# Conv filters stored in four shifted DRAM copies, so that one 128-partition transfer loads a run of ring units

## The chip, the cores and the metric

One core of a Trainium2 chip runs the whole program. The time is device microseconds of one execution; lower is better.

## The reference, cut to what matters

The input is (4, 512, 16, 32) float32, that is 2048 tokens of 512 values. Four residual layers follow one another: a mixture of 8 experts, and three convolution layers.

```
x = x + experts(_gn(x))        # top 2 of 8: silu(x w1ᵀ) * (x w3ᵀ), then w2ᵀ, weighted
x = x + conv(_gn(x), w3, w7, w15, w_mix)      # three times, each with its own weights
# conv: causal depthwise filters of 3, 7 and 15 taps over the tokens of a batch,
#   outs = [dwconv(x_flat, w) for w in (w3, w7, w15)]; y = concat(outs)
#   regrouped by 96 channels a head, then y @ w_mixᵀ (96 -> 32 channels a head)
```

A depthwise filter of k taps followed by the mix is, for one head and one group of 32 channels, a sum of k products with 32x32 matrices.

## The kernel before, in words

**Experts part.** Rows are gathered into blocks of 128 tokens, sorted by expert; there are 35 blocks, 4 or 5 for an expert. For a block g, TensorE (PE) does 48 matmuls for gate and up (L934), transposes the next block's rows (`next_rows`, L911), then `down` of the block before (L921, L924) and the transposes of `hidden` (L946). The rows of block g+1 are fetched from DRAM by GpSimd's gather ("fetch", L434); VectorE normalises them (L727); PE's L911 waits for that. GpSimd works in order: fetch, then the scatter with addition of an earlier block's result to `acc` (L443, "scatter"), then a wait until that scatter has landed (`added`), and only then the next fetch (after a copy, L432). ScalarE's L540 also waits for that landing before it fills `y_row` again.

All weights are loaded by SyncE (SP) from one queue. In its loop over experts e = 1 to 7 it issues the four w13 chunks (1024 KB each) and the two w2 halves (1024 KB each) of expert e while expert e-1 is at work; chunks 2 and 3 wait until chunks 0 and 1 have landed, the w2 halves until chunks 2 and 3 have. ScalarE (L509) and VectorE (L733) split each chunk into a high and a low part before PE uses it.

**Filters.** In the first block of each expert 1 to 7 VectorE multiplies taps and mix matrices into `filter_sb` (two chunks of 128 partitions x 12,544 bytes), splits them (L524, L763), and SP stores both chunks in DRAM (L376). In SP's program the two stores of expert e come after the w2 loads of e and ahead of the w13 loads of e+1. Partition p of a chunk is row r = p // 4 of unit p % 4; the row holds the lags of the three filters, 32 columns a lag, with zeros around them.

**Convolutions part.** Tokens are split in four phases q, so that 32 channels x 4 phases fill the 128 partitions. A head is computed in three units, each of 2, 3 or 5 windows (3, 7 or 15 taps); a window is three matmuls (L1409, L1410, L1413) whose 128x128 weights lie in `ring`, a ring buffer of 52 windows. Partitions 32q to 32q+31 of a window are the same 32 filter rows, read at an offset that moves by 32 columns with q. `load_filters` issues the loads in the order of the heads; each waits for the tasks that used its place in the ring (`head_done`). A layer has 21 tasks: heads 11 and 12 in two halves (by pair of batches), then ten whole heads, then heads 3, 4, 5 in two halves. SP first loads `rowed` of batches 0 and 1, then head 11's filters, then `rowed` of batches 2 and 3, then all other filters. PE's order in the first tasks: head 11 half 0; head 12 half 0 with a transpose (`turn`) after its first unit and, after its second, `lane_means` of the second pair of batches (L1343), for which VectorE needs that transpose's piece done and then eight `bn_stats` (L1175).

Of the kernel before, what the change touches and what calls it, by code (L numbers as in the profile page):

```python
# [6 lines left out]
P = 128  # L7
BATCH, SEQ, D, F, E = 4, 512, 512, 1024, 8
QUARTERS = SEQ // P
# [18 lines left out]
LAYERS, HEADS, HD = 3, 16, 32  # L28
SCALES = (3, 7, 15)
GROUPS = D // HD  # L30
# [7 lines left out]
SCALE_AT = (0, (SCALES[0] + 8) * HD, (SCALES[0] + SCALES[1] + 16) * HD)  # L38
LAGS = (sum(SCALES) + 8 * len(SCALES)) * HD
CHUNKS_PER_LAYER = GROUPS * HD // P  # L40
CHUNKS = 2 * (E - 1)
FILTERS_FREE = 32


def windows(s):

    return (SCALES[s] + 1) // QUARTERS + 1


def head_units(h):  # L50

    return [divmod(3 * h + m, GROUPS) for m in range(3)]


def head_runs(h):

    runs, taken = [], 0
    for s, j in head_units(h):
        if runs and runs[-1][0] == s:
            runs[-1][2] += 1  # L60
        else:
            runs.append([s, j, 1, taken])
        taken += windows(s)
    return runs
# [36 lines left out]
RING_AT, RING_AFTER, RING_COUNT = [], [], []  # L101
for _i, (_l, _h) in enumerate(HEAD_SEQUENCE):
    _at = RING_AT[-1] + head_windows(HEAD_SEQUENCE[_i - 1][1]) if _i else 0
    if _at + head_windows(_h) > RING:
        _at = 0
    _old = [_n for _n in range(_i)
            if RING_AT[_n] < _at + head_windows(_h) and _at < RING_AT[_n] + head_windows(HEAD_SEQUENCE[_n][1])]
    RING_AT.append(_at)
    RING_AFTER.append(max((_n + 1 for _n, (_layer, _head, _) in enumerate(TASKS)
                           if _old and (_layer, _head) == HEAD_SEQUENCE[_old[-1]]), default=None))  # L110
    RING_COUNT.append((_l + 1) * QUARTERS * len(head_runs(_h)))

BANKS = 5
SCALED = 2
# [16 lines left out]
def build(nc, x, gate_wT, w13T, w2T, taps, mixT, out):  # L131
    f32, f32r, i32, u32 = mybir.dt.float32, mybir.dt.float32r, mybir.dt.int32, mybir.dt.uint32
    ALU, ACT, AX = mybir.AluOpType, mybir.ActivationFunctionType, mybir.AxisListType


    acc = nc.dram_tensor("acc", [TOKENS + P, D], f32).ap()
    filters = nc.dram_tensor("filters", [HD, CHUNKS * P // HD, 2, LAGS], f32).ap()
    with ExitStack() as ctx:
        def sb(name, shape):
            return ctx.enter_context(nc.sbuf_tensor(name, shape, f32))  # L140

        ident = sb("ident", [P, P])
        group_mean = sb("group_mean", [P, P])

        filters_out = ctx.enter_context(nc.semaphore("filters_out"))
        experts_part(nc, x, gate_wT, w13T, w2T, acc, ident, group_mean, taps, mixT, filters, filters_out)
        conv_part(nc, acc, out, filters, filters_out, ident, group_mean)
# [8 lines left out]
def experts_part(nc, x, gate_wT, w13T, w2T, acc, ident, group_mean, taps, mixT, filters, filters_out):  # L156
    f32, f32r, i32, u32 = mybir.dt.float32, mybir.dt.float32r, mybir.dt.int32, mybir.dt.uint32
# [4 lines left out]
    with ExitStack() as ctx:  # L162
# [36 lines left out]
        filter_sb = late_rows[:, 0:4 * LAGS].rearrange("p (i s n) -> p i s n", i=2, s=2)  # L199
# [116 lines left out]

        block = ctx.enter_context(nc.Block(name="experts"))

        def load_w13(eng, e, k):
            eng.dma_start(w13_raw[:, k], w13T[bass.ds(e, 1), k].rearrange("o p t n -> (o p) t n"))\  # L320
               .then_inc(w13_in[k], 16)
# [26 lines left out]
        @block.sync  # L348
        def _(sp):
            for b in range(BATCH):  # L350
                sp.dma_start(rows[:, b * QUARTERS:(b + 1) * QUARTERS, 0:D], x_rows[b]).then_inc(x_in[b], 16)
            for k in range(KD):
                load_w13(sp, 0, k)

            sp.wait_ge(values_done, 1)
            for half in range(2):
                load_w2(sp, 0, half)


            sp.dma_start(taps_sb, taps).then_inc(taps_in, 16)  # L360
            sp.dma_start(mix_sb, mixT).then_inc(taps_in, 16)


            with sp.Fori(1, E) as e:
                for k in range(KD):
                    sp.wait_ge(w13_ok, (e - 1) * KD + k + 1)
                    if k >= 2:
                        sp.wait_ge(w13_in[k - 2], 16 * (e + 1))
                    load_w13(sp, e, k)
                for half in range(2):  # L370
                    sp.wait_ge(w2_ok, (e - 1) * 2 + half + 1)
                    sp.wait_ge(w13_in[KD - 2 + half], 16 * (e + 1))
                    load_w2(sp, e, half)
                for i in range(2):
                    wait_apart(sp, filter_ok, e * 2 + (i - 1), sp_passed)
                    sp.dma_start(filters[:, bass.ds(e * 8 + (4 * i - 8), P // HD)].rearrange("r a s n -> r a (s n)"),  # L376
                                 filter_sb[:, i].rearrange("p s n -> p (s n)")).then_inc(filters_out, 16)

        @block.gpsimd
        def _(pool):  # L380
# [186 lines left out]
        def _(dve):  # L567
# [37 lines left out]

            dve.sem_inc(filters_out, FILTERS_FREE)
            for b in range(BATCH):
# [135 lines left out]
            def after_first(e, g0):  # L743
                split_w2(e, g0)
                if isinstance(e, int):
                    dve.wait_ge(taps_in, 32)
                    dve.wait_ge(filter_zero, 1)
                    return
                dve.wait_ge(filters_out, e * 32 + (FILTERS_FREE - 32))
                for i in range(2):  # L750
                    c = bass.ds(e * 2 + (i - 2), 1)
                    tap = 0
                    for s, k in enumerate(SCALES):
                        at = SCALE_AT[s] + (QUARTERS - 1) * HD
                        last = nc.vector.tensor_tensor(
                            filter_sb[:, i, 1, at:at + k * HD].rearrange("p (k d) -> p k d", d=HD),
                            taps_sb[:, c, tap:tap + k].rearrange("p o k -> p (o k)")[:, :, None].to_broadcast([P, k, HD]),
                            mix_sb[:, c, s, :].to_broadcast([P, k, HD]), ALU.mult)
                        tap += k
                    last.then_inc(product_ok, 1)  # L760
                for i in range(2):
                    dve.wait_ge(filter_hi_ok, e * 2 + (i - 1))
                    nc.vector.tensor_tensor(filter_sb[:, i, 1].bitcast(f32r), filter_sb[:, i, 1], filter_sb[:, i, 0],  # L763
                                            ALU.subtract).then_inc(filter_ok, 1)
# [195 lines left out]
def conv_part(nc, acc, out, filters, filters_out, ident, group_mean):  # L960
    f32, f32r = mybir.dt.float32, mybir.dt.float32r
    ALU, ACT, AX = mybir.AluOpType, mybir.ActivationFunctionType, mybir.AxisListType
    acc_rows = acc[0:TOKENS, :].rearrange("(b p q) n -> b p q n", p=P, q=QUARTERS)
    out_rows = out.rearrange("b (p q) h w -> b p q (h w)", q=QUARTERS)
    filter_rows = filters.rearrange("r j s n -> r (j s) n")

    with ExitStack() as ctx:
        def sb(name, shape, dt=f32):
# [11 lines left out]
        ring = sb("ring", [P, RING * 2 * P], f32r)  # L980
# [24 lines left out]
        ring_in = [sem(f"ring_in{h}") for h in range(HEADS)]  # L1005
# [53 lines left out]
        @block.sync  # L1059
        def _(sp):  # L1060
            def load_rows(b):
                sp.dma_start(rowed[:, b], acc_rows[b]).then_inc(rows_in[b], 16)  # L1062

            def load_filters(i):
                l, h = HEAD_SEQUENCE[i]
                if RING_AFTER[i] is not None:
                    sp.wait_ge(head_done, RING_AFTER[i])
                for s, j0, n, taken in head_runs(h):
                    at, width = (RING_AT[i] + taken) * 2 * P, windows(s) * P
                    for q in range(QUARTERS):  # L1070
                        begin = SCALE_AT[s] + (QUARTERS - 1 - q) * HD
                        sp.dma_start(ring[HD * q:HD * (q + 1), at:at + 2 * n * width].bitcast(f32).rearrange("r (a n) -> r a n", n=width),  # L1072
                                     filter_rows[:, 2 * (l * GROUPS + j0):2 * (l * GROUPS + j0 + n), begin:begin + width]).then_inc(ring_in[h], 16)

            load_rows(0)
            load_rows(1)
            sp.wait_ge(filters_out, FILTERS_FREE + 16 * CHUNKS)
            load_filters(0)
            load_rows(2)
            load_rows(3)  # L1080
            for i in range(1, len(HEAD_SEQUENCE)):
                load_filters(i)

            stores = 0
            for tasks, first, end, bs in STORES:
                sp.wait_ge(placed, tasks)
                for b in bs:
                    sp.dma_start(out_rows[b, :, :, first * HD:end * HD], rowed[:, b, :, first * HD:end * HD]).then_inc(stored, 16)
                    stores += 1
            sp.wait_ge(stored, 16 * stores)  # L1090
# [404 lines left out]
```

## Time and profile before

| what | us |
|---|---|
| median of 3 runs | 1171.56 (1164.51 to 1361.69) |
| the profiled execution | 1166.2 |
| its span, all engines | 1164.3 |
| experts part, up to the first load of `rowed` | 745.5 |
| convolutions part | 419 |

The mean granted clock of PE in the profiled execution was 0.947 of full speed. The span is from the first to the last instruction of the profile; 1.9 us of the execution lie around it.

### The profile page before, as it was taken

What the parts mean: (1) busy time and instruction counts of PE and PEld (TensorE: products, weight loads), DVE (VectorE), ACT (ScalarE), POOL (GpSimd) and SP (SyncE); (2) the same over time, 40 slices, a digit from 0 to 9 for tenths busy, and PEclk for the clock granted to TensorE, in tenths of its full rate; (3) what the DMA queues carried; (4) which work ended last, traced back from release to release, by engine and by line L of the source; (5) the groups of instructions that cost most, each with busy time, mean ns of one, the idle gap of its engine ahead of it and who ended that gap; (6) DMA issues with size and microseconds to landing.
All of it is one profiled execution on the core that took longest, in us unless ns stands there. A gap on an engine that the chain in (4) does not pass through costs nothing. (4 is left out here: it accounts for less than half of the span.)

```text
span 1164.3 us, 14374 instructions
## 1 busy us (share of the span) xinstructions
PE 1060.9 (91%) x5234; PEld 883.5 (76%) x5235; DVE 501.3 (43%) x692; ACT 318.5 (27%) x433; POOL 128.1 (11%) x170
## 2 busy tenths in 40 slices
PE   5588999999999999999999999168999979989998
PEld 3377887887887887887878877158888968888887
DVE  5773163154245263154451452135325952387011
ACT  2403242142243242153431432012301220122112
POOL 2013111211211212111212111000000000000000
PEclk9769999999999999999999999667999989999999
DMA  8208218316415519217338140492998299698993
GB/s 361 82 19 316 48 28 314 76 27 245 138 33 196 185 18 351 39 27 278 105 112 275 27 137 18 128 238 63 205 193 182 47 220 208 127 192 168 204 207 100
DMA packets 66336, 172.72 MB, mean 148 GB/s; under 512 B 8192, under 2 KB 38016, under 8 KB 57280
## 3 DMA queue, kind: packets, MB, share of 16 engines
q1 hardware_dynamic: 58080, 149.19, 45.1%
q0 software_dynamic: 8080, 23.07, 9.4%
q8 instruction: 21, 0.34, 0.1%
q14 instruction: 11, 0.09, 0.0%
q10 hardware_dynamic: 144, 0.02, 0.0%
HBM read 136.15 MB, written 40.30 MB: 152 GB/s over the span
## 5 line engine op out<-in xcount | busy, mean ns | idle before, releaser
L1409 PE MATMUL head_ps<-split,ring 128*128 128x512 f32 (+1 forms) x630 | 225.8, 358 | 18.7 <-DMA ring<-filters 17.2
L1413 PE MATMUL head_ps<-split,ring 128*128 128x512 f32 (+1 forms) x630 | 220.2, 350 | 0.0
L1410 PE MATMUL head_ps<-split,ring 128*128 128x512 f32 (+1 forms) x630 | 219.8, 349 | 0.0
L1409 PEld LDWEIGHTS head_ps<-split,ring 128*128 128x128 f32 x630 | 123.6, 196 | 35.2 <-DMA ring<-filters 17.8
L1413 PEld LDWEIGHTS head_ps<-split,ring 128*128 128x128 f32 x630 | 123.3, 196 | 15.7
L1410 PEld LDWEIGHTS head_ps<-split,ring 128*128 128x128 f32 x630 | 123.7, 196 | 14.9
L921 PE MATMUL y_ps<-w_hi,hT_hi 128*128 128x512 f32 x280 | 117.5, 420 | 1.2 <-ACT hT_hi L534 1.2
L785 DVE TENSOR_TENSOR hidden<-silu,up_ps 128x1024 f32<-128x1024 f32 x35 | 42.7, 1219 | 165.0 <-ACT silu L552 165.0
L921 PE MATMUL y_ps<-w_lo,hT_hi 128*128 128x512 f32 x280 | 113.5, 405 | 0.0
L1236 DVE TENSOR_TENSOR stream<-stream,head_ps 128x512 f32<-128x512 f32 (+1 forms) x63 | 34.1, 557 | 176.2 <-PE head_ps L1413 176.2
L773 DVE TENSOR_TENSOR hT_lo<-hT_ps,hT_hi 128x1024 fp32r<-128x1024 f32 x35 | 42.7, 1221 | 134.0 <-ACT hT_hi L534 134.0
L552 ACT ACTIVATE silu<-gate_ps 128x1024 f32<-128x1024 f32 x35 | 35.9, 1025 | 235.5 <-PE up_ps L934 235.5
L934 PE MATMUL gate_ps<-w_hi,xT_hi 128*128 128x512 f32 x280 | 89.9, 402 | 1.7 <-DVE xT_lo L768 1.7
L443 POOL DMA_INDIRECT acc<-y_row,put x35 | 63.4, 1810 | 214.6 <-ACT y_row L540 206.3
L934 PE MATMUL up_ps<-w_hi,xT_hi 128*128 128x512 f32 x280 | 86.9, 392 | 0.0
L934 PE MATMUL up_ps<-w_lo,xT_hi 128*128 128x512 f32 x280 | 86.8, 391 | 0.0
L934 PE MATMUL gate_ps<-w_lo,xT_hi 128*128 128x512 f32 x280 | 86.7, 391 | 0.0
L934 PE MATMUL gate_ps<-w_hi,xT_lo 128*128 128x512 f32 x280 | 86.6, 391 | 0.0
L934 PE MATMUL up_ps<-w_hi,xT_lo 128*128 128x512 f32 x280 | 86.3, 390 | 0.0
L733 DVE TENSOR_TENSOR w_lo<-w_raw,w_hi 128x2048 fp32r<-128x2048 f32 x32 | 71.9, 2285 | 4.7 <-ACT w_hi L509 4.7
L924 PE MATMUL y_ps<-w_hi,hT_lo 128*128 128x512 f32 x280 | 69.3, 389 | 0.0
L921 PEld LDWEIGHTS y_ps<-w_hi,hT_hi 128*128 128x128 f32 x280 | 55.7, 199 | 12.8 <-issue 1.4
(189 smaller groups left out, 1362.8 us busy)
## 6 DMA issues: line engine op xcount, KB each, us to landing
w_raw<-in_w13T SPq DMA_DIRECT2D x32, 1024.0 KB, 11.5
ring<-filters SPq DMA_DIRECT2D x60, 480.0 KB, 10.4
filters<-rows SPq DMA_DIRECT2D x14, 1568.0 KB, 7.2
w_raw<-in_w2T SPq DMA_DIRECT2D x16, 1024.0 KB, 6.1
ring<-filters SPq DMA_DIRECT2D x84, 192.0 KB, 6.2
ring<-filters SPq DMA_DIRECT2D x48, 288.0 KB, 7.2
rows<-in_x SPq DMA_DIRECT2D x4, 1024.0 KB, 8.1
rowed<-acc SPq DMA_DIRECT2D x4, 1024.0 KB, 12.1
```

Source lines behind the costliest of these rows:

```text
L443: pool.indirect_dma_start(out=acc[:, :], out_offset=bass.IndirectOffsetOnAxis(put[:, 0:1].bitcast(u32), 0), in_=y_row[:, :], in_offset=Non ...
L552: nc.scalar.activation(silu[:, :].rearrange("p (a n) -> p a n", a=2), gate_ps[:, :, :], ACT.Silu).then_inc(silu_ok, 1)
L733: nc.vector.tensor_tensor(w13_lo[:, k], w13_raw[:, k], w13_hi[:, k].bitcast(f32), ALU.subtract).then_inc(w13_ok, 1)
L773: nc.vector.tensor_tensor(hT_lo[:, :, :], hT_ps[:, :, :], hT_hi[:, :, :].bitcast(f32), ALU.subtract).then_inc(hT_ok, 1)
L785: nc.vector.tensor_tensor(hidden[:, :].rearrange("p (a n) -> p a n", a=2), silu[:, :].rearrange("p (a n) -> p a n", a=2), up_ps[:, :, :], ...
L921: nc.tensor.matmul(y_ps[:, :], hT_hi[:, k, :], b[:, k, :], start=(k == 0 and b is w2_hi), stop=False)
L924: last = nc.tensor.matmul(y_ps[:, :], hT_lo[:, k, :], w2_hi[:, k, :], start=False, stop=(k == KF - 1))
L934: last = nc.tensor.matmul(o[:, n, :], a[:, k, :], b[:, k, t, n * 512:(n + 1) * 512], start=(k == 0 and a is xT_hi and b is w13_hi), stop=( ...
L1236: nc.vector.tensor_tensor(x, x, head_ps[n % BANKS][:, columns(pair)], ALU.add).then_inc(summed, 1)
L1409: nc.tensor.matmul(place, kernel_hi, x_hi, start=(u == 0 and a == 0), stop=False)
L1410: nc.tensor.matmul(place, kernel_lo, x_hi, start=False, stop=False)
L1413: last = nc.tensor.matmul(place, kernel_hi, x_lo, start=False, stop=(u == len(units) - 1 and a == windows(s) - 1))
```

## The change

`filters` in DRAM becomes four copies, one for each phase q, each row shifted right by 32q columns. SP stores each of the 14 chunks four times (56 stores of 1568 KB instead of 14), at the same place of its program. `load_filters` then reads all four phases at one column offset, so a run of units is one transfer to 128 partitions instead of four to 32 partitions: 54 transfers instead of 216, with the same bytes and the same contiguous pieces. Counts that are waited for follow.

```
-    filters = nc.dram_tensor("filters", [HD, CHUNKS * P // HD, 2, LAGS], f32).ap()
+    filters = nc.dram_tensor("filters", [QUARTERS, HD, ROW_OF_FILTERS], f32).ap()
...
+        def by_group(q):
+            return filters[q, :, q * HD:q * HD + CHUNKS * P // HD * 2 * LAGS].rearrange("r (a n) -> r a n", n=2 * LAGS)
...
                     wait_apart(sp, filter_ok, e * 2 + (i - 1), sp_passed)
-                    sp.dma_start(filters[:, bass.ds(e * 8 + (4 * i - 8), P // HD)].rearrange("r a s n -> r a (s n)"),
-                                 filter_sb[:, i].rearrange("p s n -> p (s n)")).then_inc(filters_out, 16)
+                    for q in range(QUARTERS):
+                        sp.dma_start(by_group(q)[:, bass.ds(e * 8 + (4 * i - 8), P // HD)],
+                                     filter_sb[:, i].rearrange("p s n -> p (s n)")).then_inc(filters_out, 16)
...
-                    for q in range(QUARTERS):
-                        begin = SCALE_AT[s] + (QUARTERS - 1 - q) * HD
-                        sp.dma_start(ring[HD * q:HD * (q + 1), at:at + 2 * n * width]...,
-                                     filter_rows[:, 2 * (l * GROUPS + j0):2 * (l * GROUPS + j0 + n), begin:begin + width])...
+                    sp.dma_start(ring[:, at:at + 2 * n * width]...,
+                                 filter_rows[:, 2 * (l * GROUPS + j0):2 * (l * GROUPS + j0 + n), SCALE_AT[s]:SCALE_AT[s] + width])...
```

## Rows read from the trace of the kernel before

**Rows 1.** The page, part 1: busy time of each engine.

```profile
PE 1060.9 (91%) x5234; PEld 883.5 (76%) x5235; DVE 501.3 (43%) x692; ACT 318.5 (27%) x433; POOL 128.1 (11%) x170
```

**Rows 2.** Waits of PE: who released it, us in total, times, longest.

```profile
PE xT_ps L911 <- DVE block_row L727: 21.6, 10, 2.9
PE head_ps L1409 <- DMA ring<-filters: 17.2, 3, 7.5
```

**Rows 3.** Timeline of SP in expert 3: start and length in us, issues.

```profile
362.12 2.24 SPq L376 DMA_DIRECT2D filters<-rows  x2
364.93 14.49 SPq L320 DMA_DIRECT2D w_raw<-in_w13T  x4
381.64 4.84 SPq L325 DMA_DIRECT2D w_raw<-in_w2T  x2
```

**Rows 4.** DMA issues at 270.5 to 272.5: count, KB, median us to landing.

```profile
filters<-rows SPq DMA_DIRECT2D x2, 1568.0 KB, 7.4
acc<-y_row,put POOLq DMA_INDIRECT x1, 12.8
```

**Rows 5.** DMA issues at 285.6 to 288, beside weight loads.

```profile
block_row<-in_x,fetch POOLq DMA_INDIRECT x1, 5.3
acc<-y_row,put POOLq DMA_INDIRECT x1, 9.0
```

**Rows 6.** DMA issues at 300.5 to 312, nothing beside them.

```profile
acc<-y_row,put POOLq DMA_INDIRECT x1, 4.8
block_row<-in_x,fetch POOLq DMA_INDIRECT x1, 3.3
```

**Rows 7.** DMA issues at 679 to 680.5, two stores and no weights.

```profile
acc<-y_row,put POOLq DMA_INDIRECT x1, 10.4
```

**Rows 8.** Timeline at 285 to 292: the fetch and PE's L911.

```profile
285.64 1.01 POOL L434 DMA_INDIRECT block_row<-in_x,fetch  x1 [0.82 <-POOL fetch L432]
...
291.75 0.66 PE L911 MATMUL xT_ps<-ident,block_row 128*128 128x128 f32 x4 [0.20 <-DVE block_row L727]
```

**Rows 9.** Timeline of PE in expert 3 and at expert 4's start.

```profile
365.21 1.11 PE L911 MATMUL xT_ps<-ident,block_row 128*128 128x128 f32 x4 [2.47 <-DVE block_row L727]
...
384.38 0.60 PE L911 MATMUL xT_ps<-ident,block_row 128*128 128x128 f32 x4
...
408.78 0.48 PE L934 MATMUL gate_ps<-w_hi,xT_hi 128*128 128x512 f32 x1
```

**Rows 10.** L921 in two stretches: length, PE and PEld busy, PEclk, DMA share, GB/s.

```profile
366.00:371.00 5.00, 4.95 (x16) 3.67 (x16) 0.77 0.98 371
...
274.00:278.00 4.00, 3.91 (x16) 2.93 (x16) 1.00 0.99 401
```

**Rows 11.** DMA from 745 to 780: GB/s in 40 slices of 0.88 us; issues.

```profile
GB/s 0 56 234 403 412 412 449 431 304 217 211 217 205 234 222 214 214 236 274 421 384 421 412 431 279 226 211 205 222 234 211 217 214 214 225 231 199 225 208 219
...
ring<-filters SPq DMA_DIRECT2D x12, 480.0 KB, 21.2
```

**Rows 12.** The chain that ended last, in order of time: issues and transfers.

```profile
926.16 0.31 SPq L1072
...
928.52 9.18 DMA ring<-filters
...
1030.45 0.31 SPq L1072
...
1031.77 11.22 DMA ring<-filters
```

**Rows 13.** Timeline of PE at the four waits of the convolutions.

```profile
778.67 0.58 PE L1409 MATMUL head_ps<-split,ring 128*128 128x256 f32 x1 [7.48 <-DMA ring<-filters]
...
789.68 0.59 PE L1343 MATMUL stat_ps<-lane,group_mean 128*128 128x4 f32 x2 [2.61 <-DVE lane L1178]
...
937.75 0.80 PE L1409 MATMUL head_ps<-split,ring 128*128 128x512 f32 x1 [6.24 <-DMA ring<-filters]
...
1043.04 0.39 PE L1409 MATMUL head_ps<-split,ring 128*128 128x256 f32 x1 [3.42 <-DMA ring<-filters]
```

**Rows 14.** Timeline of PE and VectorE, 770 to 785: around the first wait.

```profile
770.91 0.28 PE L1413 MATMUL head_ps<-split,ring 128*128 128x256 f32 x1
...
781.83 0.41 PE L1413 MATMUL head_ps<-split,ring 128*128 128x256 f32 x1
...
784.37 1.28 DVE L1175 BATCH_NORM_STATS2 bn_c<-rowed 128x6 f32<-128x512 f32 x2
```

More of the change, by code:

```diff
@@ L41 @@
 CHUNKS = 2 * (E - 1)
-FILTERS_FREE = 32
+FILTERS_FREE = 128
+ROW_OF_FILTERS = CHUNKS * P // HD * 2 * LAGS + (QUARTERS - 1) * HD
 def windows(s):
@@ L110 @@
                            if _old and (_layer, _head) == HEAD_SEQUENCE[_old[-1]]), default=None))
-    RING_COUNT.append((_l + 1) * QUARTERS * len(head_runs(_h)))
+    RING_COUNT.append((_l + 1) * len(head_runs(_h)))
 BANKS = 5
@@ L748, in after_first @@
                     return
-                dve.wait_ge(filters_out, e * 32 + (FILTERS_FREE - 32))
+                dve.wait_ge(filters_out, e * 128 + (FILTERS_FREE - 128))
                 for i in range(2):
@@ L964, in conv_part @@
     out_rows = out.rearrange("b (p q) h w -> b p q (h w)", q=QUARTERS)
-    filter_rows = filters.rearrange("r j s n -> r (j s) n")
+    phase_rows = filters.rearrange("q r n -> (q r) n")
+    begin = (QUARTERS - 1) * HD
+    filter_rows = phase_rows[:, begin:begin + CHUNKS * P // HD * 2 * LAGS].rearrange("p (j n) -> p j n", n=LAGS)
     with ExitStack() as ctx:
@@ L1069, in load_filters @@
                     at, width = (RING_AT[i] + taken) * 2 * P, windows(s) * P
-                    for q in range(QUARTERS):
-                        begin = SCALE_AT[s] + (QUARTERS - 1 - q) * HD
-                        sp.dma_start(ring[HD * q:HD * (q + 1), at:at + 2 * n * width].bitcast(f32).rearrange("r (a n) -> r a n", n=width),
-                                     filter_rows[:, 2 * (l * GROUPS + j0):2 * (l * GROUPS + j0 + n), begin:begin + width]).then_inc(ring_in[h], 16)
+                    sp.dma_start(ring[:, at:at + 2 * n * width].bitcast(f32).rearrange("p (a n) -> p a n", n=width),
+                                 filter_rows[:, 2 * (l * GROUPS + j0):2 * (l * GROUPS + j0 + n), SCALE_AT[s]:SCALE_AT[s] + width]).then_inc(ring_in[h], 16)
             load_rows(0)
             load_rows(1)
-            sp.wait_ge(filters_out, FILTERS_FREE + 16 * CHUNKS)
+            sp.wait_ge(filters_out, FILTERS_FREE + 16 * QUARTERS * CHUNKS)
             load_filters(0)
```

## The prediction

> **What bounds the kernel now.** I read the page's busy times first: PE is busy 91% of the span [rows 1], so a gain can only come from PE's idle time, and a loss from new idle time. Next the waits of PE: in the experts the largest is L911 on VectorE's L727, 21.6 us over 10 waits, and in the convolutions the loads of `ring`, 17.2 us over 3 waits [rows 2]. The change touches both regions: it makes ring loads wider, and it makes SP store 9.6 MB more in each of seven experts through the same DMA engines. So I took two stretches: SP's timeline with the landings in an expert [rows 3 to 9], and the first tasks of the convolutions with the chain of waits [rows 11 to 14].
>
> Times in an expert are counted from T, the issue of its first store (362.1 in expert 3 [rows 3], 270.6 in expert 2, 678.5 in expert 7).
>
> **Part 1, the ring loads.** Four transfers to 32 partitions become one to 128. In the slices from 745 to 780 the two `rowed` loads (128 partitions) run at 403 to 449 GB/s, and the ring loads (32 partitions) at 205 to 236 GB/s, and the slices rise to 384 to 431 for the other two `rowed` loads and fall back behind them [rows 11]. A head with 15 windows is 4 x 480 KB = 1.97 MB, so 9.1 us at 216 GB/s. For the changed load the rate is not shown: its pieces are still 1 to 2.5 KB while those of `rowed` are 8 KB, so the bounds are 216 (nothing gained) and 412 (as `rowed`). I take 412, since what differs most plainly between the two kinds is the partitions, and get 4.8 us a head. The Trainium skill (SBUF — State Buffer, Door 1: The DMA port swizzle) says that DMA bandwidth depends on how many of 16 ports the partitions reach, and that any 32 adjacent ones reach half of them; by that rule the 412 stands, and the trace's halving agrees. The same skill's DMA page is weighed under the rivals.
>
> PE waits for a ring load at three places [rows 13].
> (a) Head 12 half 0 starts at 778.67 after 7.48 us of idling. Ahead of its filters lie in the queue two `rowed` loads, head 11's filters and two more `rowed` loads: 4.19 MB of `rowed` and 3.93 MB of filters are 8.1 MB, at 412 GB/s 19.7 us from the first bytes at some 747, so 767. That is before 771.2, where PE ends head 11 [rows 14]. The wait is gone, 7.5 us. What is late next is `lane_means` at 789.68 [rows 13]: its chain starts at the transpose after the first unit of head 12, near 782 at the slow clock; VectorE's eight `bn_stats` begin at 784.4 [rows 14]. That first unit (15 matmuls) runs with 0.23 us between matmuls (778.67 to 781.83 [rows 13, 14]); without the pause PE keeps the doubled clock that it had reached before it (a matmul 0.28 us long instead of 0.41 [rows 14]), some 1.4 us more. PE's second unit lies under VectorE's work. I count 8.9, with 7.5 as the lower end.
> (b) Head 13 of layer 1: the load is issued at 926.16 when the task is done that frees its place, and the last quarter lands at 937.7 (928.52 + 9.18), 11.5 us later [rows 12]. One transfer at 412 GB/s: about 2.2 us before bytes flow (the 11.5 less 9.1, rounded down for the three issues saved) and 4.8, so 933.2. PE had ended the task before at 931.5 (937.75 - 6.24): 1.7 us of idling instead of 6.2, gain 4.5. After the old pause ten matmuls ran at half clock; whether 1.7 us of idling avoids that is open, 0 to 1.8 us more, taken as 0.
> (c) Head 12 half 0 of layer 2: issue 1030.45, landing 1043.0, PE idle 3.42 us [rows 12, 13]. New landing 1037.5, ahead of 1039.6: gain 3.4.
> All other ring loads land before they are needed now, and will do so sooner: nothing. The 162 issues saved are SP's time only, which hides behind PE. Sum of part 1: -16.8 us, bounds 0 and -18.7.
>
> **Part 2, the stores.** Each expert 1 to 7 gets six more stores of 1.6 MB. With nothing but stores in flight DMA moves 401 GB/s (274 to 278 [rows 10]): 4.0 us each. The eight stores last to about T+1.2+32 = T+33, and with the GpSimd transfers between them T+36. Two things are behind them.
>
> *The weights of the next expert* are issued behind the stores. Before, chunk 2 had landed when the first w2 half was issued, T+19.5, and chunk 3 when the second was, T+24.4 (381.64 + 4.84 [rows 3]). Six stores at 4.0 with some sharing shift them by 25, to T+44.5 and T+49.4. PE starts the next expert at T+46.7 in the short experts (408.78 - 362.12 [rows 3, 9]) and takes 2.8 us a chunk, so it wants chunk 3 at T+55.1, less 4.2 for the two splits: T+50.9. It fits by 1.5 us, and by 5 when the stall below has moved PE; chunk 2 by 3.6 more. w2 is wanted a block later. Cost 0; this cover is thin, and from where it fails is the second rival.
>
> *GpSimd's fetch and scatter* share the DMA engines. The scatter of T+0.7 lands 12.8 us after issue beside two stores and then weights [rows 4], 10.4 with two stores alone [rows 7], 9.0 beside weights [rows 5], 4.8 with nothing [rows 6]. GpSimd waits for it, then fetches 1.6 us later, and this fetch lands 5.3 us after issue beside weights [rows 5], 3.3 with nothing [rows 6]. In expert 2 that chain is exactly as long as PE's work: fetch 285.64, landed 290.9, L727 (0.6 us) and L911 at 291.75 after a wait of 0.2 [rows 8]. So there is no cover left in front of L911, and now stores stand where weights stood.
> The scatter: the part after the two stores was 12.8 - 10.4 = 2.4 us; stores of 1568 KB instead of chunks of 1024 make that 3.6 at most, so 12.8 to 14.0; I take 13.2, nearer to the measured end. The fetch beside stores is not shown: the lower bound is 5.3 (as beside weights), the upper is the clear 3.3 plus the whole 7.7 that stores add to a scatter, 11; I take the middle, 8.2. L911 then comes at 0.7 + 13.2 + 1.6 + 8.2 + 0.8 = T+24.5. Before, it came at T+22.3 (384.38 - 362.12 [rows 3, 9]) in five of the seven experts, where the 2.5 us wait at the expert's first L911 was followed by slow clock, and at T+21.0 in the other two (291.75 less 0.2 and 270.6 [rows 8]). Stall: 5 x 2.2 + 2 x 3.5 = 18 us.
> The clock: after a wait of 2.5 us (365.21 [rows 9]) the sixteen L921 that follow had a granted clock of 0.77 and took 4.8 us instead of 3.7 [rows 10]. In the seven experts this came to 0, 0, 1.1, 1.1, 1.2, 1.6 and 1.6 us (one of either kind in rows 10). The new stall is of the same length and stands before the same L921: +6.6 us again, +8 with the transposes.
> The second fetch of an expert: scatter issued at T+17.4, landed T+31, fetch T+32.2 to T+40.5, L911 at T+41.3 against a need of T+24.5+17.7+1 = T+43: covered by 2 us. Later ones are in the clear. Expert 7 has no weights behind its stores, but the same first chain. Its stores end near T+36 = 715, long before 745.
> VectorE's wait on `filters_out` is for the expert before, done for 30 us. ScalarE's wait for the same scatter (L540) has its result needed only by `down`, behind L911. Sum of part 2: +26 us; with both terms at their lower bounds L911 comes at T+21.2 and the cost is 0; at their upper ones it comes at T+27.9, 6 us late seven times, and with the clock the cost is 50.
>
> **Sum.** 1166.2 (the profiled execution) - 16.8 + 26 = 1175.4. I say 1175. The profiled execution lies 5 us under the median of the three runs and 2 us over the fastest, so the comparison is with 1166.
>
> **The rivals.**
> *First: the fetch isn't held up by stores more than by weights.* If packets of the two queues strictly take turns, a fetch of few packets waits for a few packets of the other queue, whatever is queued behind. Then 0.7 + 12.8 + 1.6 + 5.3 + 0.8 = T+21.2: no stall in five experts and 0.2 us in two. Result 1166 - 17 = 1149. For it: fetches move only from 3.3 to 5.3 us while DMA is saturated. Against: scatters go from 4.8 to 12.8. The Trainium skill (DMA: Bandwidth & Descriptors, Queues, rings and completion order) has the engines go round-robin between queues at packet granularity, which is this case; the 12.8 us speaks for a longer hold than that. Chance 0.17.
> *Second, slower: the weights come late.* The mechanism: w13 of the next expert is behind eight stores in one queue. It decides from where the last store lands later than about T+42: then in the three short experts (4 blocks) PE waits for w13 one for one. Were a store to take 6.5 us (the four copies scatter rows over 90 MB, and shifted rows don't start where the old ones did), the last lands at T+54, 21 us behind my T+33, so chunk 3 at T+66 to 67 is 11 to 12 us late three times (with the stall counted) and up to 2 us in the three long experts: 1175 + 40 = 1215. For it: the two stores' landings differ by 5.3 us now, not 4.0. Against: 401 GB/s in the stretch that holds only stores. At 5.3 the last lands at T+42.7, and the cost is 2 to 4 us. Chance 0.12.
> *Third, slower: a long hold.* Both upper bounds of part 2 hold, +50: 1166 - 17 + 50 = 1199. Chance 0.10.
> *Fourth: wide ring loads are no faster,* because pieces of 1 to 2.5 KB are what slows them. Then only (a few) issues are saved: 1166 + 26 - 2 = 1190. The Trainium skill (DMA: Bandwidth & Descriptors, Rules for kernel authors) says that transfers to disjoint partition halves merely serialise on the same 16 engines; taken alone that leaves no bandwidth to be gained by widening. The trace's factor of two between the kinds of load speaks against it. Chance 0.05.
> My forecast, with 1163 to 1188 around it: 0.56.
>
> **How the numbers follow.** The forecast is the likeliest, so its 1175 is the predicted time. The range runs from the first rival to the third, 1149 to 1199; beyond it are the second rival and the tails. About 2% (23 us) is what a measurement of this kernel tells from no change: 1143 and 1189 are the borders. Faster by more: only if the first rival comes with gains that I don't see, 0.07. Slower by more: the second, third and half of the fourth rival, and a tail of the forecast, 0.25. Within: 0.68.
>
> **What would show it.** Right: no wait of head 12 half 0 for `ring` near 771, slices above 380 GB/s during ring loads, `lane_means` of pair 1 some 44 us after the first `rowed` issue less 9; one wait of 2 to 4 us at the second L911 of each expert 1 to 7, released by L727 and behind it a fetch that takes 7 to 9 us; no wait of L509 for w13. Wrong: fetches near 5 us and no such wait (first rival); L509 or L934 waiting for w13 (second); ring slices near 216 (fourth). The least certain term is the fetch beside stores: each us of it costs 7.

## The result, and the profile after

The changed kernel takes 1171.0 us (median of 20 runs; all but one between 1168.5 and 1174.0), the kernel before 1166.7 in as many runs beside it: a ratio of 1.0035 [1.0026, 1.0044], so 4.1 us more. The forecast had both effects with their signs, but 9 us more as their sum (1175.4 against 1166.2). The profiled execution took 1169.6 (its span 1167.7). Line numbers of the functions below are 6 higher than before.

| profiled execution, us | before | after | change | forecast |
|---|---|---|---|---|
| start to the first load of `rowed` | 745.5 | 767.5 | +22.0 | +26 |
| from there to the end | 418.8 | 400.2 | -18.6 | -16.8 |

**The convolutions.** DMA, 767 to 800 (40 slices of 0.83 us), answers to [rows 11]:

```profile
GB/s 0 119 119 417 367 457 407 367 407 407 410 413 416 403 442 430 427 397 437 407 358 405 395 397 397 394 394 397 397 394 394 391 261 28 12 0 0 0 0 0
...
ring<-filters SPq DMA_DIRECT2D x3, 1920.0 KB, 20.7
rowed<-acc SPq DMA_DIRECT2D x4, 1024.0 KB, 10.1
```

The slices with ring loads hardly differ any more from those with `rowed` loads: mostly 390 to 440 GB/s instead of 205 to 236. The waits of PE, which answer to [rows 2]:

```profile
PE xT_ps L917 <- DVE block_row L733: 34.4, 16, 2.8
...
PE head_ps L1415 <- DMA ring<-filters: 2.0, 1, 2.0
...
PE gate_ps L940 <- DVE w_lo L739: 1.5, 2, 1.1
```

Of three waits for `ring` one is left. The first line shows the price: 16 waits instead of 10, and 12.8 us more. The third is new. PE in the convolutions, which answers to [rows 13]:

```profile
802.92 0.59 PE L1349 MATMUL stat_ps<-lane,group_mean 128*128 128x4 f32 x2 [3.92 <-DVE lane L1184]
...
946.61 0.50 PE L1415 MATMUL head_ps<-split,ring 128*128 128x512 f32 x1 [1.99 <-DMA ring<-filters]
...
1043.87 0.49 PE L1391 MATMUL stat_ps<-partial,whole 128*128 128x128 f32 x2 [0.21 <-DVE partial L1255]
```

`lane_means` comes 35.45 us after the first `rowed` load (before 44.2): 8.8 less. The last line ends a stage that both kernels have just before place (c); its row of before is

```profile
1035.29 0.49 PE L1385 MATMUL stat_ps<-partial,whole 128*128 128x128 f32 x2 [0.21 <-DVE partial L1249]
```

289.83 us into the part then, 276.40 now: 13.4 less, of which 8.8 was (a), so (b) gave 4.7; its wait fell from 6.24 us to 1.99. The remaining 5.2 of the 18.6 came at (c).

**The experts.** SP in expert 3, which answers to [rows 3], and the DMA issues at 271 to 274 and at 286 to 289, which answer to [rows 4] and [rows 5]:

```profile
366.52 10.09 SPq L382 DMA_DIRECT2D filters<-rows  x8
377.18 2.19 SPq L325 DMA_DIRECT2D w_raw<-in_w13T  x2
```

```profile
filters<-rows SPq DMA_DIRECT2D x3, 1568.0 KB, 9.5
acc<-y_row,put POOLq DMA_INDIRECT x1, 12.6
...
block_row<-in_x,fetch POOLq DMA_INDIRECT x1, 8.9
acc<-y_row,put POOLq DMA_INDIRECT x1, 12.3
```

The scatter takes 12.6 (before 12.8), the fetch behind it 8.9 (before 5.3). The chain in expert 2 (T = 271.65), which answers to [rows 8]:

```profile
285.50 0.18 POOL L438 COPY fetch<-from_row 128x1 int32 x1 [10.72 <-DMA acc<-y_row,put]
286.50 1.01 POOL L440 DMA_INDIRECT block_row<-in_x,fetch  x1 [0.82 <-POOL fetch L438]
...
295.56 0.55 DVE L733 TENSOR_SCALAR block_row<-block_row,row_value 128x512 f32<-128x512 f32 x1 [7.60 <-DMA block_row<-in_x,fetch]
...
296.16 0.66 PE L917 MATMUL xT_ps<-ident,block_row 128*128 128x128 f32 x4 [1.92 <-DVE block_row L733]
```

L917 starts at T+24.5 and not at T+21.2 as before. In the seven experts, from the timelines of PE and SP:

| expert | 1 | 2 | 3 | 4 | 5 | 6 | 7 | sum |
|---|---|---|---|---|---|---|---|---|
| second L911 of before, at T+ | 22.4 | 21.2 | 22.3 | 22.4 | 20.9 | 22.4 | 22.5 | |
| second L917 of after, at T+ | 24.2 | 24.5 | 24.5 | 24.5 | 24.5 | 24.5 | 24.5 | |
| later by | 1.8 | 3.3 | 2.2 | 2.1 | 3.6 | 2.0 | 2.0 | 17.1 |
| its wait | 1.7 | 1.9 | 1.9 | 1.9 | 1.9 | 1.9 | 1.9 | 13.1 |
| expert (T to next T) longer by | 1.8 | 3.3 | 3.9 | 3.7 | 4.2 | 3.6 | 2.2 | 22.7 |

The first T is 0.7 earlier, hence 22.0 in all. Where an expert grew by more than its L917 moved, the clock or VectorE is behind it. The sixteen L927 that follow the second wait in experts 3 and 2 (windows: length, PE, PEld, PEclk, DMA share, GB/s), beside [rows 10]:

```profile
391.00:397.00 6.00, 5.52 (x16) 4.07 (x16) 0.72 1.02 383
296.00:302.00 6.00, 3.91 (x16) 2.93 (x16) 1.00 1.02 385
```

Both had waited 1.9 us; one took 1.6 us longer (a mean granted clock of 0.72, so over half of the window at the level of 1.2 GHz), the other kept 2.4 GHz. From the second L917 to the third it is 19.4 and 19.3 us in experts 3 and 4 and 17.8 in the other five, so these two lost 3.2 us together. And VectorE ahead of expert 7 shows the new third wait:

```profile
672.66 0.55 DVE L733 TENSOR_SCALAR block_row<-block_row,row_value 128x512 f32<-128x512 f32 x1 [2.44 <-DMA block_row<-in_x,fetch]
673.12 4.49 DVE L739 TENSOR_TENSOR w_lo<-w_raw,w_hi 128x2048 fp32r<-128x2048 f32 x2
```

VectorE splits two chunks of w13, then normalises the rows of the fetch, then splits two more. A late fetch now holds up the last two splits, and PE waits 1.14 us here and 0.38 in expert 6.

### The profile page after: what moved, and what is told of

It reads as the page before. It is cut to its first block and busy times, and to the rows that moved or that the text cites. A ratio compares the mean times of both kernels' runs of the same rounds, so it can differ in the third digit from the quotient of the medians.

```text
span 1167.7 us, 14338 instructions
## 1 busy us (share of the span) xinstructions
PE 1063.5 (91%) x5234; PEld 883.1 (76%) x5235; DVE 501.8 (43%) x692; ACT 319.1 (27%) x433; POOL 132.5 (11%) x170
## 2 busy tenths in 40 slices
DMA packets 69791, 240.14 MB, mean 206 GB/s; under 512 B 6272, under 2 KB 36096, under 8 KB 55360
## 5 line engine op out<-in xcount | busy, mean ns | idle before, releaser
L1415 PEld LDWEIGHTS head_ps<-split,ring 128*128 128x128 f32 x630 | 121.6, 193 | 19.4 <-DMA ring<-filters 2.2
L1419 PEld LDWEIGHTS head_ps<-split,ring 128*128 128x128 f32 x630 | 121.3, 193 | 15.9 <-DVE split L1233 0.2
L1416 PEld LDWEIGHTS head_ps<-split,ring 128*128 128x128 f32 x630 | 121.7, 193 | 14.9
L927 PE MATMUL y_ps<-w_hi,hT_hi 128*128 128x512 f32 x280 | 121.6, 434 | 1.2 <-ACT hT_hi L540 1.2
L927 PE MATMUL y_ps<-w_lo,hT_hi 128*128 128x512 f32 x280 | 117.5, 420 | 0.0
L779 DVE TENSOR_TENSOR hT_lo<-hT_ps,hT_hi 128x1024 fp32r<-128x1024 f32 x35 | 42.7, 1221 | 146.0 <-ACT hT_hi L540 146.0
L940 PE MATMUL gate_ps<-w_hi,xT_hi 128*128 128x512 f32 x280 | 90.2, 403 | 3.2 <-DVE xT_lo L774 1.7
L940 PE MATMUL up_ps<-w_hi,xT_hi 128*128 128x512 f32 x280 | 86.9, 392 | 0.0
L940 PE MATMUL gate_ps<-w_lo,xT_hi 128*128 128x512 f32 x280 | 86.7, 391 | 0.0
L940 PE MATMUL up_ps<-w_lo,xT_hi 128*128 128x512 f32 x280 | 86.7, 391 | 0.0
L940 PE MATMUL gate_ps<-w_hi,xT_lo 128*128 128x512 f32 x280 | 86.4, 390 | 0.0
L940 PE MATMUL up_ps<-w_hi,xT_lo 128*128 128x512 f32 x280 | 86.3, 389 | 0.0
L927 PEld LDWEIGHTS y_ps<-w_hi,hT_hi 128*128 128x128 f32 x280 | 58.1, 208 | 13.7 <-issue 1.4
## 6 DMA issues: line engine op xcount, KB each, us to landing
filters<-rows SPq DMA_DIRECT2D x56, 1568.0 KB, 17.1
w_raw<-in_w13T SPq DMA_DIRECT2D x32, 1024.0 KB, 12.8
```

Source lines behind the costliest of these rows:

```text
L779: nc.vector.tensor_tensor(hT_lo[:, :, :], hT_ps[:, :, :], hT_hi[:, :, :].bitcast(f32), ALU.subtract).then_inc(hT_ok, 1)
L927: nc.tensor.matmul(y_ps[:, :], hT_hi[:, k, :], b[:, k, :], start=(k == 0 and b is w2_hi), stop=False)
L940: last = nc.tensor.matmul(o[:, n, :], a[:, k, :], b[:, k, t, n * 512:(n + 1) * 512], start=(k == 0 and a is xT_hi and b is w13_hi), stop=( ...
L1415: nc.tensor.matmul(place, kernel_hi, x_hi, start=(u == 0 and a == 0), stop=False)
L1416: nc.tensor.matmul(place, kernel_lo, x_hi, start=False, stop=False)
L1419: last = nc.tensor.matmul(place, kernel_hi, x_lo, start=False, stop=(u == len(units) - 1 and a == windows(s) - 1))
```

## The experiments

Each was timed beside the kernel before (1166.7 to 1167.6). "Start" is the start of the convolutions part in the profiled execution, "part" its length. Both are of one execution: the changed kernel, e1 and e3 have the same experts part, and it took 767.5, 771.7 and 769.0 us. The profiled execution of e4 (1166.4) is its fastest by 6.5 us.

| kernel | us | ratio [95%] | start | part |
|---|---|---|---|---|
| before | 1166.7 | 1 | 745.5 | 418.8 |
| after | 1171.0 | 1.0035 [1.0026, 1.0044] | 767.5 | 400.2 |
| e1 stores only | 1191.1 | 1.0198 [1.0181, 1.0215] | 771.7 | 420.2 |
| e2 wide loads only | 1147.2 | 0.9826 [0.9809, 0.9842] | 746.6 | 399.1 |
| e3 loads of 64 | 1193.3 | 1.0231 [1.0198, 1.0265] | 769.0 | 423.0 |
| e4 six stores late | 1173.9 | 1.0059 [1.0041, 1.0077] | 765.1 | 399.4 |
| e6 stores spread | 1149.5 | 0.9854 [0.9825, 0.9884] | 746.0 | 399.1 |
| e7 e4, rows last | 1150.9 | 0.9860 [0.9843, 0.9876] | 748.6 | 400.4 |
| e8 half pieces | 1146.9 | 0.9840 [0.9814, 0.9866] | 746.5 | 397.9 |
| e9 e7 + e8 | 1146.3 | 0.9823 [0.9807, 0.9840] | 744.9 | 400.1 |
| e10 after, rows last | 1168.8 | 1.0012 [1.0001, 1.0023] | 770.6 | 399.6 |
| e11 e8, rows last | 1147.6 | 0.9839 [0.9825, 0.9853] | 745.1 | 399.2 |

**The two halves of the change alone.** e1 keeps the four copies and loads 32 partitions at a time:

```
-                    sp.dma_start(ring[:, at:at + 2 * n * width]..., filter_rows[:, ...]
+                    for t in range(4):
+                        sp.dma_start(ring[32 * t:32 * (t + 1), at:at + 2 * n * width]..., filter_rows[32 * t:32 * (t + 1), ...]
```

> Four stored copies as in the changed kernel, but each run of the ring is loaded by four transfers to 32 partitions as before. Theory: the experts lose what they lose in the changed kernel (22 us up to the first load of rowed) by GpSimd's scatter and fetch standing behind stores, and the convolutions gain nothing: 1167 + 22 = 1189 us, ring slices near 216 GB/s, PE waits of 7.5, 6.2 and 3.4 us for ring. Rival: the convolutions gained by how the copies lie in DRAM or by fewer conflicts there, not by the width of a transfer; then ring loads are faster here too and the time is nearer to 1171.

e2 stores one copy, as before, and loads 128 partitions in one transfer:

```
+    filter_rows = filters.rearrange("r (c j) s n -> (r c) (j s) n", c=QUARTERS)
...
+                    j = (l * GROUPS + j0) % 11
+                    sp.dma_start(ring[:, at:at + 2 * n * width]..., filter_rows[:, 2 * j:2 * (j + n), ...]
```

> One stored copy as before, and the ring loaded by 128-partition transfers whose rows are taken from wrong places of that copy (the output is not the reference's; pieces, bytes and real filter values are kept). Theory: the experts part is that of before (745.5 us to the first load of rowed), the convolutions part that of the changed kernel (400 us instead of 419): 1167 - 18.6 = 1148 us. Rival: the gain of the convolutions needs the experts' changed timing or the four copies in DRAM; then less than half of the 18.6 us appears.

The wide loads alone give 19.8 us, the stores alone cost 24.2 (by their medians, against 1167.0). The sum, +4.4, is within the error what the change does (+4.1), so the two effects add up. The waits for `ring` in e1 are 16.5 us over 3, in e2 2.4 over 1, near those before (17.2 over 3) and after (2.0 over 1). In e1 the slices with ring loads stay at 172 to 242 GB/s, and in e2, with one copy in DRAM, they run mostly at 380 to 450: how the copies lie in DRAM isn't what makes the loads fast.

**What makes the wide load fast.** e3 makes two transfers of 64 partitions out of one of 128 (the diff is e1's with 2 and 64).

> The changed kernel with each run of the ring loaded by two transfers to 64 partitions (0 to 63, 64 to 127). If what counts is how many of the ports the partitions reach, 64 adjacent partitions are as bad as 32: ring slices near 216 GB/s, the three waits of PE for ring back, 1171 + 18.6 = 1190 us. If the rate follows the number of partitions or the number of transfers, it is in between or as with 128 partitions: 1171 to 1180 us, slices well above 300 GB/s.

Its part is 423.0 us, PE waits 20.5 us over 3 for `ring`, and the slices from 767 to 800 (40 of 0.83 us) have the rates of before:

```profile
GB/s 0 0 0 99 129 427 437 377 437 457 343 199 164 205 214 211 220 223 223 214 202 279 191 337 417 437 367 427 346 204 163 200 192 192 211 223 214 211 220 202
...
ring<-filters SPq DMA_DIRECT2D x6, 960.0 KB, 28.9
```

Half as many transfers as in e1 and twice the bytes and partitions in each, at the same 200 to 220 GB/s: neither the number of transfers nor their size sets the rate, and it doesn't grow with the partitions from 32 to 64. That it depends on which partitions a transfer reaches is not shown by that alone; 64 partitions out of both halves (0 to 31 and 64 to 95) in one transfer were not tried. The Trainium skill (SBUF — State Buffer, Door 1: The DMA port swizzle) says that partitions 0 to 63 reach the same half of the ports as 0 to 31; the 200 to 220 GB/s of both kinds agree.

**Where the stores stand.** e4 stores the unshifted copy at T, and the other three behind the weights of the next expert:

```
+            weights(1)
+            with sp.Fori(1, E - 1) as e:
+                stores(e, range(1), True)
+                weights(e + 1)
+                stores(e, range(1, QUARTERS), False)
+            stores(E - 1, range(QUARTERS), True)
```

> The changed kernel, but SP issues only the copy q = 0 of both chunks ahead of the next expert's weights and the other six stores behind them (all eight at once for expert 7). Theory: the first scatter and fetch of an expert stand beside two stores and weights as before the change, later ones have some 17 us of cover, so only expert 7 still loses 2 to 3 us: 1167 - 18.6 + 3 = 1151 us, PE's second L917-like wait gone in six experts. Rival: the loss comes from the amount written (DRAM or DMA time taken as such), wherever it stands; then the six stores cost some 3 us an expert here too and the time stays near 1170 us.

It missed by 23 us. The second wait of an expert is gone in six experts as expected, but (waits of PE)

```profile
PE xT_ps L931 <- DVE block_row L747: 23.7, 10, 2.9
PE gate_ps L954 <- DVE w_lo L753: 14.2, 3, 5.7
```

PE waits 3.4, 5.7 and 5.1 us for the low part of w13, as it starts on the next expert behind each of the three short ones. The first of them on VectorE's timeline:

```profile
405.48 4.54 DVE L753 TENSOR_TENSOR w_lo<-w_raw,w_hi 128x2048 fp32r<-128x2048 f32 x2 [1.29 <-ACT w_hi L529]
414.25 0.55 DVE L747 TENSOR_SCALAR block_row<-block_row,row_value 128x512 f32<-128x512 f32 x1 [4.23 <-DMA block_row<-in_x,fetch]
414.71 4.49 DVE L753 TENSOR_TENSOR w_lo<-w_raw,w_hi 128x2048 fp32r<-128x2048 f32 x2
```

w13 was there: ScalarE had made the high parts of all four chunks by 410.9. VectorE sat idle for 4.2 us on the fetch, which lands 8.6 us after its issue beside the moved stores, with two splits queued behind it. It is the third wait of the changed kernel, grown. Two kernels test that reading. e7 is e4 with the order of VectorE changed:

```
             def new_expert(e, g0):
-                split_w13(e, g0, range(KD // 2))
+                split_w13(e, g0)
                 normalise_rows(g0 + 1)
-                split_w13(e, g0, range(KD // 2, KD))
```

> As the run with six late stores, with one more change: in a new expert VectorE splits all four w13 chunks before it normalises the next block's rows, instead of two chunks, rows, two chunks. Theory: the fetch beside stores is as late as before, but the splits no longer wait for it, so PE's three waits for w13's low part (14.2 us) go and the time is 1174 - 14 - some us of half clock = 1153 to 1158 us. Rival: w13 comes late by itself, behind stores; then the waits for it stay and the time stays near 1174 us.

The three waits are gone and the time is 1150.9, a little below the range given. By the medians that is 23 us under e4, by the profiled executions 15.5; the three waits were 14.2. e6 leaves that order, but stores only one more copy behind the weights, and two once the third chunk of the next expert is split (expert 7's units 48 to 55, which no layer reads, are stored once):

```
+                stores(e, range(1), True)
+                weights(e + 1)
+                stores(e, range(1, 2), False)
+                sp.wait_ge(w13_ok, (e + 1) * KD + 3)
+                stores(e, range(2, QUARTERS), False)
+            stores(E - 1, range(1), True)
```

> As the run with six late stores, but only one copy (two stores) directly behind the weights, the last two copies (four stores) when the next expert's third w13 chunk has been split, and of expert 7, whose filters are never read, one copy alone. Theory (from the run with six late stores, where VectorE waited 4.2 us for a fetch between two splits of w13 and PE then for w13's low part, 14.2 us over 3 waits): no fetch that VectorE needs soon stands beside stores, so those three waits go, and expert 7 loses nothing: 1167 - 18.6 + 1 to 3 = 1150 us. Rival: writing 4 copies costs DMA or DRAM time that something pays for wherever it stands: 1160 to 1174 us.

1149.5: as expected. 50 of the 56 stores, in the same DMA engines, now cost some 2 us over e2's 1147.2; all 56 at T cost 24.

**How a store holds the fetch.** e8 leaves all stores at T, but cuts each in two, so that a piece is 6272 bytes and not 12,544:

```
                     for q in range(QUARTERS):
+                        for part in range(2):
+                            sp.dma_start(by_group(q)[:, ..., part * LAGS:(part + 1) * LAGS],
+                                         filter_sb[:, i, part]).then_inc(filters_out, 16)
```

> The changed kernel with every store cut in two (high part, low part), so that its contiguous pieces have 6272 bytes instead of 12,544 and there are 112 stores of 784 KB; order and bytes are the same. If GpSimd's transfers are held behind a number of queued pieces and then take turns with them piece by piece, the hold halves: the first fetch of an expert lands 5.5 to 6.5 us after its issue instead of 8.9, the first scatter after 9 to 10.5 instead of 12.5, PE's second wait of an expert (1.9 us, seven times) goes with most of its half clock, and the time is 1171 - 15 = 1156 us. If the hold goes by bytes or by the saturation of the engines, nothing changes: fetch near 8.9, 1171 us.

1146.9, 9 us under the 1156 expected: by the medians all of the stores' cost is gone (e2, with one copy stored, takes 1147.2). GpSimd on the timeline of expert 2 (T = 270.48), and PE:

```profile
271.19 2.40 POOL L450 DMA_INDIRECT acc<-y_row,put  x1 [14.98 <-ACT y_row L547]
281.51 0.18 POOL L439 COPY fetch<-from_row 128x1 int32 x1 [7.92 <-DMA acc<-y_row,put]
282.52 1.01 POOL L441 DMA_INDIRECT block_row<-in_x,fetch  x1 [0.82 <-POOL fetch L439]
...
291.32 0.60 PE L918 MATMUL xT_ps<-ident,block_row 128*128 128x128 f32 x4
```

The scatter lands 9.7 us after issue instead of 12.6, the fetch 7.9 instead of 8.9, so the chain is 3.9 us shorter and L918 doesn't wait. But half of the reason that I gave, a hold that goes by the number of queued pieces, falls. The queues served (q0 is GpSimd's, q1 SP's; packets, MB, share of 16 engines; a packet of a store is one piece), first from the issue of the changed kernel's scatter, 272.4 to 279.1, the next 0.4 us, and 279 to 285; then of its fetch, 286.5 to 292.7:

```profile
q1 hardware_dynamic: 224, 2.61, 95.6%
...
q1 hardware_dynamic: 10, 0.13, 82.0%
q0 software_dynamic: 8, 0.02, 22.4%
...
q1 hardware_dynamic: 174, 1.98, 80.5%
q0 software_dynamic: 144, 0.26, 23.8%
...
q1 hardware_dynamic: 208, 2.41, 95.4%
q0 software_dynamic: 10, 0.04, 1.6%
```

and of e8, from its fetch, 282.5 to 287.9, and from its scatter, 276.5 to 278.0 and 278.0 to 278.5 (271.2 to 276.5 shows 352 packets of q1 alone, 2.01 MB):

```profile
q1 hardware_dynamic: 411, 2.28, 102.0%
...
q1 hardware_dynamic: 64, 0.40, 96.8%
...
q0 software_dynamic: 47, 0.10, 105.0%
```

For 6.9 us after its issue no packet of the scatter is served in the changed kernel, and for 6.8 in e8; for the fetch it is 5.6 (the ten packets up to 292.7 begin at 292.1) and 5.4. In that time 13 and 11 whole pieces an engine pass, or 24 and 23 halves (packets under 512 bytes left out), but 2.3 to 2.7 MB in each case. So this wait doesn't go by the number of pieces. Whether it goes by bytes or by time these two kernels can't tell, as DMA moves some 400 GB/s in both, and it is no constant: in the kernel before, beside weight loads (pieces of 8 KB), the fetch of 285.64 has its first packet 3.9 us after issue, behind 1.5 MB. The queues from 288 to 289 and over the whole fetch, 285.64 to 291:

```profile
q1 hardware_dynamic: 54, 0.44, 104.5%
...
q1 hardware_dynamic: 244, 1.74, 86.2%
q0 software_dynamic: 80, 0.26, 13.4%
```

What does halve is the time from the first packet to the landing of a scatter, 5.7 us (279.3 to 285.0) and 2.9 (278.0 to 280.9). In it the two queues share the engines: beside the scatter's 144 packets 158 whole pieces pass in the changed kernel (1.98 MB), and some 115 halves in e8 (0.72 MB). With nothing beside them a fetch has its first packet 1.7 us after issue and a scatter 2.2; in the kernel before, 300.5 to 302.5 and 302.5 to 303:

```profile
q0 software_dynamic: 68, 0.21, 38.4%
...
q0 software_dynamic: 16, 0.03, 119.3%
```

The 68 are the rest of the 80 packets of the fetch issued at 298.38; the 16 are the first of the scatter issued at 300.51.

The Trainium skill (DMA: Bandwidth & Descriptors, Queues, rings and completion order) has each engine drain typically some 9 to 17 descriptors of one ring, and 64 at most, before it switches. The changed kernel's 11 and 13 lie in the typical range, e8's 23 and 24 above it and under the ceiling, so a fixed count of descriptors doesn't describe the wait. What sets it is open.

**Combinations.** e9 is e7 with halved pieces and expert 7 stored once.

> Six late stores, w13 split ahead of the rows, stores cut in two and expert 7 storing one copy alone, all together. Theory: only smaller remains of the experts' loss are left, 1148 to 1151 us, the convolutions part 399 to 400 us and the experts part within 3 us of the kernel before. Rival as for the others: the amount written costs time wherever it stands, 1160 us or more.

e10 is the changed kernel with VectorE's order of e7, e11 is e8 with it.

> The changed kernel, but VectorE splits all four w13 chunks of a new expert before it normalises the next block's rows (it did two chunks, the rows, two chunks). Theory (the order in VectorE is what made PE wait for the weights' low part, 0.38 and 1.14 us, and not a late w13): both waits go, the sixteen other waits of PE for block_row stay as they are, and the time falls by 1.5 us, to a ratio of 1.002 to the kernel before. Rival (the rows are wanted as urgently as the splits): the waits of PE for block_row grow by up to 4.5 us in each of seven experts and the time rises. Second rival (w13 lands late): the two waits stay.

> The kernel with every store cut in two, and with VectorE splitting all four w13 chunks ahead of the next block's rows. Theory (the halved pieces took away the second wait of each expert, and the only new waits left are 1.29 and 0.96 us behind a fetch that VectorE takes between the splits): these two go, 2.2 us less than 1146.9, so 1144.7, a ratio of 0.982 to the kernel before. Rival (the waits come back elsewhere, in the next expert's first L911 that waits for its fetch anyway): 1146 to 1147, ratio 0.984.

e9 at 1146.3 is the fastest by its median, with e8 within the error of it: both beat the kernel before by 20 us. In e10 the two waits for w_lo are gone and the 16 for block_row stay (36.0 us, longest 3.5); its ratio of 1.0012 is 2.3 thousandths under the changed kernel's, some 2.7 us where 1.5 was expected. Its own profiled execution is the slowest of its runs, so it doesn't show where the rest is. e8 still has waits of 2.2 us for w_lo; in e11 they are gone too, but the time is that of e8 within its error, as the rival had it.

## Why the prediction was off

The path was right in both parts and two terms of the sum were mis-sized, the clock behind the new waits in the experts and what (c) gives. Since the net is the small difference of two effects of some 20 us, errors of 4.0 and 1.8 us in them made +9.2 out of +3.4 (profiled executions).

**Part 2, in size: +22.0 and not +26.** There is one new wait at the second L917 of each expert 1 to 7, at T+24.5 in six and T+24.2 in one (forecast T+24.5). The scatter took 12.6 (forecast 13.2) and the fetch 8.9 (8.2): that their sum came out within 0.1 us is luck. The weights came in time, the first w2 half being issued at T+45.9 (forecast T+44.5), and L940 never waited for w13 itself.
- *The stall*, 18: L917 moved by 17.1. Only 13.1 of it shows as waiting, mainly since in experts 2 and 5 too, 1.6 and 1.7 us of the lower clock now come ahead of the wait and are covered by it.
- *The clock* is the term that failed: "the new stall is of the same length and stands before the same L921: +6.6 us again, +8 with the transposes". The stall was 1.9 us and not 2.5, and was followed by the lower clock in two experts of seven, for 3.2 us; with what remains unassigned of the 22.7 (22.7 - 17.1 - 3.2 - 1.5 = 0.9) at most 4.1. I had taken for certain what is not. Nor does the length of the pause alone decide it. The distance from one transpose L911 (L917) to the next shows it, 19.1 to 19.6 us with the lower clock and 17.7 to 18.0 without: in the kernel before, five of seven waits of 2.4 to 2.5 us were followed by it, in the changed kernel all seven of the same length, and in e6 one of 3.0 us was not. Over all twelve traces it is 64 of 83 after waits of 2.4 to 2.6 us and 8 of 26 after waits of 1.4 to 2.0. What decides is open.
- *VectorE's order*, 1.5 us, was not in the sum. I said that no step waits for w13, and had looked at SP's queue behind the stores but not at what is queued on VectorE behind the fetch. It is small here, 14 us in e4, and e10 takes it away.
- 26 - 0.9 - 3.9 + 1.5, less the 0.7 that the first T is earlier, is the 22.0.
- Three slips in the prediction's numbers move its sum by less than 1 us: the upper bounds make T+28.1 and not T+27.9, stores add up to 8.0 us to a scatter (12.8 - 4.8) and not 7.7, and eight stores of 5.3 us from T+1.2 end at T+43.6 and not T+42.7.

**Part 1, in size: -18.6 and not -16.8.** (a) 8.8 against 8.9, (b) 4.7 against 4.5. Whether 1.7 us of idling at (b) would spare PE the lower clock had been left open: the 1.99 us that it waited didn't, the next 4.4 us having a granted clock of 0.65 (before, 0.53 in 4.3 us). (c) is the term that was too small: 5.2 against 3.4. I counted the pause of 3.4 us and not what followed it. PE in the kernel before right behind that pause, and in the changed kernel at the same work (windows: length, PE busy, PEclk, DMA share, GB/s):

```profile
1043.00:1047.80 4.80, 4.76 (x27) 0.64 1.05 220
```

```profile
1048.20:1053.00 4.80, 4.80 (x42) 1.00 0.52 195
```

27 matmuls in 4.8 us at a clock of 0.64, 42 at full clock: 1.7 us, which with 3.4 makes the 5.2. At (a) I had counted this, and here not.

**How far the split holds.** It is that of one execution of each kernel. By the medians of e1 and e2 the stores cost 24.2 us and the wide loads give 19.8, against 26 and 16.8: then it is the second part that missed by more, 3.0 us against 1.8. Which part missed by more is thus not settled. The two terms are steadier: a second wait was followed by the lower clock in two experts of seven in e1 and e3 too.

Both misses go the same way by either count; the forecast of 1175.4 stands against 1169.6 of the profiled execution. The sign, and that the kernel stays within 2%, held. Of the rivals, the first (no hold by stores) is refuted by a fetch of 8.9 us, the second by L940's lack of a wait for w13, the third by T+24.5, the fourth by the slices of 390 to 440 GB/s.

## What to carry to other kernels

Before a bulk transfer is put into a busy kernel, look for small transfers with an in-order chain behind them (scatter, fetch, normalise, transpose): here 9.6 MB of stores an expert cost 3.5 us each time at one place in SP's program, and almost nothing at another place or in pieces of half the size. When a transfer becomes late, list what is queued behind its reader on its own engine too: two weight splits behind a wait for rows cost e4 more than its stores did. And price what the clock may do behind each pause, not only the pause, but as a chance: waits of one length were followed by the lower clock in some experts and not in others.

## What the runs showed of the hardware

- Transfers to 64 adjacent partitions run no faster than to 32: 200 to 220 GB/s, against 390 to 440 for 128 (e3, after).
- Behind queued stores the first scatter of expert 2 has its first packet served 6.9 and 6.8 us after its issue and the fetch behind it 5.6 and 5.4, after 2.3 to 2.7 MB of the other queue, whether these are pieces of 12,544 or of 6272 bytes (after, e8). From there to its landing the scatter takes 5.7 us beside the larger pieces and 2.9 beside the smaller. With nothing beside them the first packet comes 2.2 us (scatter) and 1.7 us (fetch) after issue (before).
- Waits of PE of 2.4 to 2.6 us were followed by a stretch at the lower clock level in 64 of 83 cases, waits of 1.4 to 2.0 us in 8 of 26 (all traces), at a cost of some 1.6 us each; the length of the wait alone doesn't decide.
